# Constant multiplications ahead of TensorE's picks and sends in three passes of a graph network kernel

## The reference, cut to what matters

```python
x = x + segment_sum(h_rel[src, type16] * weight1, dst)                 # layer 0
x = x + relu(Tx0 @ W0 + Tx1 @ W1 + Tx2 @ W2 + b)                        # layer 1
        # Tx1 = prop(Tx0); Tx2 = 2 * prop(Tx1) - Tx0
        # prop(v) = segment_sum(w_hat[:, None] * v[src], dst)
x = x + attention over edges with 86 relation types                     # layer 2
x = x + segment_sum(h[src], dst) / max(degree, 1)                       # layer 3
```

## Time and profile before

| | |
|---|---|
| time, median of 3 runs | 7825.96 us (7807.99 to 7840.15) |
| profiled execution, span from first to last instruction | 10430.0 us |
| TensorE matmul busy in it | 5347.8 us (51%) |
| VectorE busy | 4782.2 us (46%) |
| GpSimd busy | 5362.5 us (51%) |
| mean granted TensorE clock over the span | 0.597 |

### The profile page before, as it was taken

The page is one execution under the profiler, slowest core; times in us unless marked ns, Lnnn a source line. Parts: engine busy times, 40 slices in busy tenths (PEclk is TensorE's granted clock), DMA queues, the critical chain, the costliest instruction groups (busy, mean ns, idle before and its releaser), DMA issues. The chain is left out here.

```text
span 10430.0 us, 148696 instructions
## 1 busy us (share of the span) xinstructions
PE 5347.8 (51%) x40755; PEld 4389.9 (42%) x40756; DVE 4782.2 (46%) x15556; ACT 2574.5 (25%) x8163; POOL 5362.5 (51%) x5577
## 2 busy tenths in 40 slices
PE   4232322232355666656566555555555555556666
PEld 2121222222244444544444444555555545455555
DVE  4444444454456666544444443333333333346665
ACT  4334333333311111123333333111111111121111
POOL 3565555556465555444444443555555555535554
PEclk8555555555566666656666665555555555557777
DMA  5000000000111111134344343111111111112222
GB/s 130 11 11 11 11 11 11 11 10 11 20 38 39 40 40 40 35 100 140 128 141 140 131 139 117 29 30 29 29 31 30 30 30 30 30 33 61 62 62 52
DMA packets 463914, 542.70 MB, mean 52 GB/s; under 512 B 219393, under 2 KB 373025, under 8 KB 463709
## 3 DMA queue, kind: packets, MB, share of 16 engines
q0 software_dynamic: 178288, 148.77, 8.8%
q1 hardware_dynamic: 228973, 178.17, 6.6%
q10 hardware_dynamic: 56448, 213.62, 5.2%
HBM read 293.47 MB, written 246.66 MB: 52 GB/s over the span
## 5 line engine op out<-in xcount | busy, mean ns | idle before, releaser
L709 POOL DMA_INDIRECT arena<-table,ibuf x3328 | 3144.7, 945 | 2571.7 <-issue 1124.4
L709 POOL DMA_INDIRECT arena<-nodes,ibuf x2240 | 2215.1, 989 | 2387.0 <-DVEq L1563 1532.3
L1105 PE MATMUL ps_agg<-mem_a,arena 128*32 128x80 f32 (+1 forms) x3904 | 513.4, 317 | 801.3 <-DVEq L1550 724.6
L1569 DVE TENSOR_TENSOR big<-big,ps_agg 32x80 f32 (+1 forms) x488 | 113.0, 232 | 1687.6 <-PE ps_agg L1105 857.4
L1105 PE MATMUL ps_agg<-mem_b,arena 128*32 128x80 f32 (+1 forms) x3904 | 543.6, 307 | 667.5 <-DVEq L1550 386.4
L1366 PE MATMUL ps_agg<-tbuf,msg 128*64 128x80 f32 x2496 | 373.5, 344 | 936.4 <-DVE msg L2020 861.6
L1105 PEld LDWEIGHTS ps_agg<-mem_a,arena 128*32 128x32 f32 (+1 forms) x3904 | 453.1, 162 | 864.1 <-DVEq L1550 734.1
L1105 PEld LDWEIGHTS ps_agg<-mem_b,arena 128*32 128x32 f32 (+1 forms) x3904 | 436.1, 154 | 751.6 <-DVEq L1550 411.8
L832 ACT ACTIVATE tbuf<-O,tbuf 128x49 bf16<-128x49 bf16 x2176 | 625.3, 365 | 495.3 <-DVE H L1709 307.3
L1366 PEld LDWEIGHTS ps_agg<-tbuf,msg 128*64 128x64 f32 x2496 | 335.9, 226 | 958.1 <-DVE msg L2020 877.0
L1794 DVE TENSOR_SCALAR tbuf<-iota,at_f 128x256 bf16<-128x256 bf16 x2940 | 621.8, 294 | 105.5 <-remote 85.9
(11 more groups left out here) (388 smaller groups left out, 12225.4 us busy)
## 6 DMA issues: line engine op xcount, KB each, us to landing
table<-tbuf ACTq DMA_DIRECT2D x294, 544.5 KB
idx_a<-lows_d SPq DMA_DIRECT2D x602, 192.0 KB
arena<-table,ibuf POOLq DMA_INDIRECT x3328
table<-tbuf ACTq DMA_DIRECT2D x98, 495.0 KB
arena<-nodes,ibuf POOLq DMA_INDIRECT x2240
table<-tbuf SPq DMA_DIRECT2D x25, 1024.0 KB, 4.3
idx_a<-lows_d SPq DMA_DIRECT2D x86, 224.0 KB
nodes<-O SPq DMA_DIRECT2D x7, 224.0 KB, 3.0
```

The costliest lines, as they stand in the source:

```text
L709: nc.gpsimd.indirect_dma_start(out=INTO[s][:, k, c, 0:WIDTH[s]], out_offset=None, in_=TABLE[s], in_offset=bass.IndirectOffsetOnAxis(ap=ibu ...
L1105: last = nc.tensor.matmul(ps_agg[ROW0[s]:ROW0[s] + CHN[s], 0:WIN], narrow[:, k, c, 0:CHN[s]], onehots[b][:, c, :], start=(c == 0), stop=(c ...
L1569: V.tensor_tensor(into, into, ps_agg[r0:r1, 0:WIN], ALU.add)
```

## The change

A helper issues `n` matmuls of a 128x32 stationary constant with the 256 columns of `iota2`. Their results go to PSUM partitions of the block sum's bank that no one reads (96 to 127 of `ps_t`). In pass 2 partitions 96 to 127 of `ps_agg` are in use, so there the result goes to the partitions 0 to 31 of the block sum itself: before a block's first send with `start`, so that the send overwrites it, and later as a product with zeros that is added to the open sum. Two of them (five at the first batch of a block) stand ahead of each send, behind the wait for `s_sbadd` and ahead of the waits for `s_to` and `s_slot`; three stand ahead of each pick except in step 0, ahead of the pick's waits. Nothing is removed or moved. The entry `3` of `unused_sums` is not used by any call.

```diff
         block_sums = {1: ps_t, 2: ps_agg, 4: ps_t}
+        unused_sums = {1: ps_t[SPLIT:P, 0:W2], 2: ps_agg[0:D, 0:W2], 3: ps_agg[SPLIT:P, W2:2 * W2], 4: ps_t[SPLIT:P, 0:W2]}
+        zeros_h = zero[:, :].bitcast(BF16)[:, 0:1].to_broadcast([P, D])
...
+            def stay_busy(n, s, open_group=False):
+                for _ in range(n):
+                    nc.tensor.matmul(unused_sums[s], zeros_h if open_group else ident_h[:, 0:D], iota2[:, :],
+                                     start=not open_group, stop=not open_group)
...
                     if q == 0:
                         pe.wait_ge(s_sbadd, (BEFORE[h] + e + 1) + i * UNIT[s])
                         carry_wait(pe)
+                    stay_busy(2 if q else 5, s, s == 2 and q > 0)
                     if s == 4:
                         pe.wait_ge(s_to, (e * NBATCH + q + 1) + i * (UNIT[s] * NBATCH))
                         carry_wait(pe)
...
                         sums = s == 2 and q % 4 == 3 and (q >= 7 or not first)
+                        if q:
+                            stay_busy(3, s, s == 2)
                         if q + 3 < NBATCH or not last:
                             pick(i, f, q + 3, sums)
...
                         for q in range(NBATCH):
+                            if q:
+                                stay_busy(3, s, s == 2)
                             if q + 1 < NBATCH or e + 1 < UNIT[s] or not last:
                                 pick(i, f * UNIT[s] + e, q + 1)
                             send(i, f * UNIT[s] + e, q)
```

## The result

| | before | after |
|---|---|---|
| median of the runs | 7832.11 us (5 runs, 7807.99 to 7846.38) | 7868.92 us (5 runs, 7865.65 to 7869.98) |
| ratio, 95% interval | | 1.0054 (1.0043 to 1.0065) |

The change makes the kernel 0.5% slower, where 7718 us were forecast. Nothing was gained in any pass.

What follows compares the result with a forecast made beforehand. No engine bounds it; stages wait on each other above a gather floor of 7480 us. Of 346 us above it, 170 gained less 47 for first sends and 15 for switching saves 108: 7826 to 7718 us, range 7580 to 7880.

Steps and rivals of the forecast that it cites:

- If the clock stays at 1.0 in the three passes, their TensorE busy time falls by the cold share: Passes 1, 2 and 4: full clock cuts TensorE's busy time by 306, 431 and 122 us, together 859 in the profile.
- With a faster TensorE these waits go until the gathers are the limit: GpSimd's waits for freed slots (885 us in pass 2) hang on TensorE's group product and vanish down to the gathers' pace.
- 49% are 170, if they are spread as in the profile: Passes 1, 2 and 4 hold 49% of the plain run's 346 us above the gathers' bound: 170 us to gain.
- the floor: Whole kernel: 5568 gathers at 1.245 us plus start, gaps between passes and end give at least 7480 us.
- The doubt that the prediction named as its largest: Whole profile: recording stalls leave TensorE idle, so a plain run's clock may already be better than the profile says.
- hidden anyway: Rival, chance 0.24: the three passes already stand at the gathers or VectorE; 7826 us, 7800 to 7850.
- The clock: Passes 1, 2 and 4: granted clock rises from 0.64, 0.63 and 0.77 to 1.0, except perhaps at pass 1's 4.9 us wait.
- The price of a constant: Each added 256-column matmul on TensorE takes 0.22 us at the low clock or 0.11 at the high one.
- The five of the first send: Five constants behind each block's wait for `s_sbadd` are all on the path: 47 us, 95 at the low clock.
- The switch of shape: Changing the stationary from 128x128 to 128x32 costs TensorE about 0.11 us; at most 280 us, 15 on the path.
- The floor is none: Rival, chance 0.13: gathers take less without recording, TensorE sets the pace; half the gain gives 7456 us.
- Slower: Rival, chance 0.16: the clock stays and constants cost 0.22 us each, mainly in pass 2; 8007 us, at worst 8121.

Runs made afterwards that it cites:

- b1_pass1: Changed kernel with the constants kept in pass 1 alone: 7836.90 us, ratio 1.0016 to the kernel before.
- b2_pass2: Changed kernel with the constants kept in pass 2 alone (1040 matmuls): 7856.46 us, ratio 1.0038 to the kernel before.
- d1_pass2_short: Changed kernel with constants in pass 2 alone, shortened from 256 to 32 columns, on the first kind of chip: 7856.65 us, ratio 1.0047 to the kernel before.
- h1_wide_short: Changed kernel with constants in pass 2 alone, 96-column stationary, 32 columns moved, first kind of chip: 7849.69 us, ratio 1.0029 to the kernel before.
- c3_pass2_short: Changed kernel with constants in pass 2 alone, shortened from 256 to 32 columns, on the second kind of chip: ratio 1.0061 to the kernel before.
- e2_wide_short: Changed kernel with constants in pass 2 alone, 96-column stationary, 32 columns moved, second kind of chip: ratio 1.0047 to the kernel before.
- e1_wide: Changed kernel with constants in pass 2 alone, 96-column stationary, 256 columns moved, second kind of chip: ratio 1.0056 to the kernel before.
- b0_before: The kernel before, run again with the change undone: 7823.86 us, ratio 0.9992 to the kernel before.

## Why the prediction was wrong

Its forecast, 7718 us, is 151 under the time measured. Step by step:

- **The step that failed** is "If the clock stays at 1.0 in the three passes, their TensorE busy time falls by the cold share", and with it the gain taken from it, "With a faster TensorE these waits go until the gathers are the limit". TensorE did not get faster. In pass 2, the only one with slack, the clock went from 0.72 to 0.80, and the constants cost more time than it gave back: TensorE's busy time rose from 965.9 to 1036.5 us, GpSimd's wait for freed slots from 256.5 to 277.0, and the pass from 1314 to 1338. With twice the constants the clock was 0.88 and the busy time 1074. The prediction took the clock's gain whole, put the constants' cost at 47 us of first sends and 15 of switching, and took the rest as covered; in pass 2 idle time covered 47 of 71 us. Its second half, that a TensorE with less to do shortens the waits, was never put to a run of its own; the three profiles without constants above go its way.
- **The size of the slack.** "49% are 170, if they are spread as in the profile": they were not. The 49% came from stretches full of the standstills of its chip. On the other kind the span is 7828.9, and with the node gathers at their mean of 0.996 the floor is 141 + 3328 x 1.245 + 2240 x 1.296 + 310 between passes + 53 = 7550, so 278 are above it: 236 in pass 2, 28 in passes 0 and 3, none in pass 1 and 17 in pass 4. In passes 1 and 4 there was nothing to gain. The doubt that the prediction named as its largest was the right one, and it should have moved the chance of "hidden anyway" up.
- **The median for a mean.** The earlier trace rows give the gather's median, 0.944; the page gives a mean of 0.996 for those from node rows, which are 2240 of them: 117 us of floor that were counted as slack. The shorter gaps between passes on the other kind of chip, 310 us for 349, take 39 of it back.
- **The clock** was to rise to 1.0. It rose to 0.79, 0.80 and 0.97, from 0.71, 0.72 and 0.93. The Trainium skill ("TensorE: Matmul & The Clock Gate", HAM oscillation) holds that pauses bring the clock down and steadier work keeps it up. The traces agree in direction for the long constants: in pass 2 the clock was 0.71 to 0.74 without any, 0.80 with 1040 and 0.88 with 2080. With 1040 short ones it was 0.74, no more than in `b1_pass1` without any. No dose that ran held it at 1.0.
- **The price of a constant** was right. Five ahead of a send in pass 1, after the change, then that send (TensorE in order of time: start, us, instruction, count, idle before):

```profile
2609.11 0.71 PE L1113 MATMUL ps_t<-iota,ident_h 128*32 128x256 bf16 x5 [1.84 <-DVE big L1820]
2609.74 1.14 PE L1236 MATMUL ps_t<-tbuf,mem_a 128*96 128x256 bf16 x7
```

  Less the last one's 0.27, four take 0.44: 0.11 each at full clock.
- **The five of the first send**, 47 us on the path, are not found. The wait for L1808 in pass 1 was 121.5 us on the first chip and 51.8 on the other kind, 48.9 with the change, and the pass has the same length with them. In passes 1 and 4 they stand where the gathers bind; what those of pass 2 cost by themselves (14 us by the same price) was not told apart.
- **The switch of shape** was put at 0.11 each, 15 us on the path. In pass 2 the median from a pick to the constant behind it, start to start, is 0.106 us in `b2_pass2` and 0.117 in `d1_pass2_short`, where the constant is 128x32, and 0.026 in `h1_wide_short`, where it is 128x96: 0.08 to 0.09 for the switch. From a short constant to the send behind it, it is 0.119 us in `c3_pass2_short` against 0.081 in `e2_wide_short`. The Trainium skill ("TensorEngine Tiling (Array Packing)", section Key Properties) says that a change of tiling mode drains TensorE; the traces agree that the change costs time and do not show whether it is a drain. `h1_wide_short`, with the constants in the sends' shape, still loses 0.29%.
- **The rivals.** "Hidden anyway" describes passes 1 and 4 as they are. "The floor is none" is excluded: pass 1 stayed at 1075 us with 0.08 more clock. "Slower" had the right pass and the right sign for the wrong reason: it wanted the clock to stay and each constant to be paid at 0.22 us, 181 us in all. The clock rose, and a pass with an eighth of the columns lost as much.

**What stays open.** Why the losses are equal for different constants, why a turn comes at 51 or at 54.6 us in the mean, and whether the clock falls because of the long turn or the long turn comes from the lower clock, no run here shows. No run raised the clock without adding work. A price of the places that is not the shape's was not tested on a chip of the first kind. Long constants in the sends' shape (`e1_wide`) were never timed on a chip of the first kind. The 0.16% of `b1_pass1` has no place in its profile. No version was faster than the kernel before, which remains the best.

## What to carry to other kernels

Ask first which passes have slack above their own bound, with mean durations and on a profile whose span agrees with the timed runs; a profile a third longer than the median is of another regime, and its idle time is not yours to win. A clock raised by added work is worth something only if TensorE's busy time falls, so look at that and not at the clock: here the clock went from 0.72 to 0.88 in the pass with all the slack, the busy time from 962 to 1074 us, and the pass got longer. When a loss doesn't change with the dose, cut the pass into its turns, and do it at two different instructions, since one cut can hide an uneven pair.

## What the runs showed that I had not expected

- **Two kinds of chips.** The same kernel took 7823 us on one and 10443 or 10605 on another, and an edit has another price on the second: 1040 short constants cost 0.47% on the first kind and 0.61% on the second, 2080 long ones 0.35% and 1.27%.
- **Two lengths of a turn** in the kernel before, 51.3 and about 54.6 us, and after the change an uneven pair of 52.4 and 56.8 us that one cut hides and another shows.
- **Equal idle time.** Without constants TensorE's idle time in pass 2 is 350, 352 and 353 us in passes of 1318, 1314 and 1291 us.
- **A constant runs beside a gathered group.** In `b2_pass2` constants of 128x32 lie between the group's products on other partitions, and start 0.05 us from them, while each takes 0.23 us and more:

```profile
4001.36 0.28 PE L1115 MATMUL ps_agg<-iota,zero 128*32 128x256 bf16 x1
4001.42 0.23 PE L1107 MATMUL ps_agg<-mem_a,arena 128*32 128x80 f32 x1
4001.47 0.27 PE L1115 MATMUL ps_agg<-iota,zero 128*32 128x256 bf16 x1
4001.49 0.30 PE L1107 MATMUL ps_agg<-mem_a,arena 128*32 128x80 f32 x2
```

- **The gathers from node rows** take 0.052 us more in the mean than their median, and those from the table 0.003. 643 of the 2240 take more than 1.0 us, up to 1.61, as in this row of `b0_before` (min, median, longest in ns; first and last start).

```profile
L709 POOL DMA_INDIRECT arena<-nodes,ibuf x2240: 938/945/1613, 2293.3 to 7775.7; - x187
```
